# Moving the zero fill of the top-4 layer's slots from SyncE's queue to GpSimd's own queue in the first attention

## The reference, cut to what matters

```python
q = (x @ wq).reshape(Bq, Tq, N_KV, N_REP, HEAD_DIM)
k_lat = (x @ wk_down).reshape(Bq, Tq, N_KV, D_LAT)
v_lat = (x @ wv_down).reshape(Bq, Tq, N_KV, D_LAT)
...
scores = jnp.einsum('bqhrd,bkhd->bhrqk', q, k) * scale
scores = jnp.where(causal, scores, jnp.finfo(scores.dtype).min)
probs = jax.nn.softmax(scores, axis=-1)
y = jnp.einsum('bhrqk,bkhd->bqhrd', probs, v)
```

## Time and profile before

| | us |
|---|---|
| median of 3 runs | 1745.87 (1744.73 to 1747.52) |
| profiled execution | 1749.62 |
| its span on the core | 1747.7 |
| POOL busy in the span | 790.3 (45%) |
| PE / DVE / ACT busy in the span | 1187.7 / 1022.0 / 672.2 |
| first attention's units (first to last remainder on POOL) | 243.21 to 418.33 |

### The profile page before, as it was taken

One profiled execution on the slowest core, in us unless ns is written; L12 is line 12 of the kernel. 1 busy time (PEld: TensorE's weight loads), 2 busy tenths in 40 slices (PEclk: granted clock), 3 DMA queues, 4 the chain that ended last, 5 costly groups with the idle time before them and its releaser, 6 DMA issues.

```text
span 1747.7 us, 31813 instructions
## 1 busy us (share of the span) xinstructions
PE 1187.7 (68%) x10584; PEld 865.1 (50%) x10585; DVE 1022.0 (58%) x2671; ACT 672.2 (38%) x1035; POOL 790.3 (45%) x989
## 2 busy tenths in 40 slices
PE   2198568876199208598976448888885075989772
PEld 2198546654199203497962213444433034979620
DVE  6546656766546884142565757887766941335533
ACT  2154246664044102253531126766672022535310
POOL 0524435553423347666667522222200377666676
PEclk9999689997599559799997758999895587999986
DMA  9233134430133001454641100000000013646422
GB/s 363 65 94 111 38 104 144 151 123 2 36 95 87 25 24 49 130 191 161 192 128 49 42 14 2 2 0 0 0 1 1 24 49 120 198 156 199 145 60 62
DMA packets 100089, 150.10 MB, mean 86 GB/s; under 512 B 21520, under 2 KB 54928, under 8 KB 99216
## 3 DMA queue, kind: packets, MB, share of 16 engines
q1 hardware_dynamic: 58768, 75.30, 13.1%
q0 software_dynamic: 20480, 41.98, 8.1%
q10 hardware_dynamic: 20736, 31.47, 5.4%
HBM read 74.16 MB, written 74.45 MB: 85 GB/s over the span
## 4 chain that ended last, share of the span: by engine, by line
PE 26%; POOL 25%; DVE 16%; issue 14%; DMA 10%; SPq 4%; ACT 3%; DVEq 0%; ACTq 0%; POOLq 0%
POOL slots_top L624 15%; POOL AREA L1098 10%; PE PS L845 5%; DMA slots_top<-XN,ROW 4%; DMA AREA<-results_top,ROW 4%; SPq L1346 3%; PE PS L298 3%; PE PS L300 2%; PE PS L299 2%; PE PS L1789 2%; DVE AREA L1961 2%; DVE XN L407 2%; PE PS L1776 2%; PE PS L1764 2%; DMA query_rows<-AREA 1%
## 5 line engine op out<-in xcount | busy, mean ns | idle before, releaser
L624 POOL DMA_INDIRECT slots_top<-XN,ROW x320 | 317.4, 992 | 365.3 <-DVE ROW L578 225.0
L1098 POOL DMA_INDIRECT AREA<-results_top,ROW x320 | 304.6, 952 | 243.2 <-issue 87.8
L1009 DVE SCALAR_TENSOR_TENSOR AREA<-PS,AREA 128x512 f32<-128x512 f32 x96 | 66.4, 692 | 233.9 <-ACT AREA L983 209.8
L908 PE MATMUL PS<-WGU,AREA 128*128 x768 | 186.2, 386 | 0.0
L1961 DVE TENSOR_REDUCE AREA<-PS 128x4 f32<-128x1024 f32 x128 | 156.8, 1225 | 38.9 <-PE PS L1764 36.6
L1881 ACT ACTIVATE AREA<-PS,AREA 128x1024 f32<-128x1024 f32 x128 | 142.8, 1116 | 87.2 <-PE PS L1776 85.1
L908 PEld LDWEIGHTS PS<-WGU,AREA 128*128 128x128 f32 x768 | 141.4, 194 | 16.7 <-ACT AREA L972 0.7
L1379 POOL TENSOR_TENSOR AREA<-AREA 128x1536 f16<-128x1536 f32 x32 | 92.9, 2903 | 99.9 <-ACT AREA L1594 99.9
L417 PE MATMUL PS<-IDF,XN 128*128 128x128 f32 x192 | 48.7, 411 | 129.5 <-DVE XN L407 129.5
L930 PEld LDWEIGHTS PS<-WD,AREA 128*128 128x128 f32 x768 | 100.2, 191 | 12.7 <-DVE AREA L1004 8.2
L930 PE MATMUL PS<-WD,AREA 128*128 x768 | 102.0, 276 | 6.3 <-DVE AREA L1004 6.3
(11 more groups left out here) (257 smaller groups left out, 3147.4 us busy)
## 6 DMA issues: line engine op xcount, KB each, us to landing
AREA<-slots_top SPq DMA_DIRECT2D x96, 256.0 KB
results_top<-AREA ACTq DMA_DIRECT2D x96, 256.0 KB
slots_top<-ZERO SPq DMA_DIRECT2D x24, 512.0 KB, 3.1
AREA<-slots_top SPq DMA_DIRECT2D x48, 128.0 KB
results_top<-AREA ACTq DMA_DIRECT2D x48, 128.0 KB
AREA<-query_rows SPq DMA_DIRECT2D x48, 128.0 KB, 2.9
slots_top<-XN,ROW POOLq DMA_INDIRECT x320, 2.2
AREA<-results_top,ROW POOLq DMA_INDIRECT x320, 2.5
```

The costliest lines, as they stand in the source:

```text
L624: nc.gpsimd.indirect_dma_start(out=L.xs[q], out_offset=bass.IndirectOffsetOnAxis(ap=ROW[:, n:n + 1], axis=0), in_=XN[:, t * D:(t + 1) * D] ...
L908: ins = nc.tensor.matmul(o, XTF[:, v, j * P:(j + 1) * P], w, start=True, stop=True)
L1009: nc.vector.scalar_tensor_tensor(out=HF[:, v, :4 * P].rearrange("p (j h) -> p j h", h=P), in0=got, scalar=1.0 / SX, in1=HA[:, :4 * P].rear ...
L1098: nc.gpsimd.indirect_dma_start(out=slots[L.tag][u][:, c * D:(c + 1) * D], out_offset=None, in_=L.ys[g * GT // L.tiles], in_offset=bass.Ind ...
```

## The change

SP no longer issues the 24 pieces; POOL does, each behind the remainder of the unit of the same number. The tile, the destinations, the size of a piece and the semaphore stay. POOL's DMAs go through a queue of their own ("software dynamic" in the profile, q0) and SP's through another (q1).

```diff
@@ attn0_sync
                     max_row(t + 1)
                 if q_batch(t, 1) is not None:
                     q_write(q_batch(t, 1))
-                if 0 <= t < ZERO_PIECES["top4"]:
-                    zero_slots(sp, L1, t)
 
@@ attn0_pool
                 wait(pool, a_pv, u - 1)
                 nc.gpsimd.tensor_tensor(PB0[1][:, u % 2, :], PF[:, u % 2, :], PB0[0][:, u % 2, :], ALU.subtract
                                         ).then_inc(a_plo.sem, 1)
+                if u < ZERO_PIECES["top4"]:
+                    zero_slots(pool, L1, u)
```

## The result

| | before | with the change |
|---|---|---|
| median, 20 runs each | 1746.56 us | 1753.4 us |
| ratio, 95% interval | | 1.0043 (1.0026 to 1.0059) |
| span of the profiled execution | 1747.7 us | 1750.5 us |
| first to last remainder on POOL (start to start) | 172.2 us | 183.1 us |

The change made the kernel slower by 0.43%, some 7 us; 1744.7 and no change that can be told had been forecast, with a range that ended at 1750.0.

What follows compares the result with a forecast made beforehand. Mostly POOL's indirect DMAs bound the kernel; only the SP leg at 240 to 420 us could change. Terms -1.5 - 0.9 - 0.2 + 1.4 = -1.2 us gave 1744.7 us, 8-in-10 range 1737.5 to 1750.0.

Steps and rivals of the forecast that it cites:

- What bounds the kernel: Chain of waits: only the stage from 240 to 420 us can change, on a leg of SP's DMAs, then PE and ACT.
- 24 issues leave SP: First attention, SP's queue: of 24 zero pieces only three stand on the chain, so moving them gives -1.5 us.
- the three terms that a clean SP queue was given: SP's queue in the first attention: issues -1.5, landings of writes -0.9, rows of maxima -0.2 us.
- The first rival: First attention: SP is the pacemaker, 0.30 us per unit over 23 units, -6.9 us, time 1739.0; chance 0.35.
- Lighter queue: SP's queue without 512 KB pieces: seven query writes land sooner, -0.9 us, and rows of maxima, -0.2 us.
- POOL's DMAs at 0 us: 24 added issues on POOL, 1.3 us each, fit into 2.78 us free per unit, so cost 0.
- The zeros' bytes beside the queries: Seven query writes on the chain share DMA engines with pieces, 0.2 us each: +1.4 us, bounds 0 and +5.6.
- The price of full sharing: Delay of a query write that shares the DMA engines with a zero piece all the way: 0.8 us.
- Slower: contention on the whole SP leg: Zeros delay the write and again the read or rows, 0.8 + 0.8 us per leg: +8.6, time 1754.5; chance 0.11.
- POOL as the bound: First attention: POOL issues over 2.8 us would pace the stage; at 3.1 us +7.4 less 2.6, time 1750.7; chance 0.04.
- The sign of being wrong in kind: Time changing outside 240 to 420 us by more than a microsecond would show the prediction wrong in kind.
- the contention's bound for the writes alone: Upper bound of sharing by seven query writes: +5.6 - 2.6 = +3.0 us, used for the range's end at 1750.0.

Runs made afterwards that it cites:

- second trace of the kernel before: The kernel before, unchanged, traced again on the same chip as the change and SP behind the loop; first to last remainder 170.8 us, median 1744.12 us.
- SP behind the loop: Against the kernel before, SP issues all 24 zero pieces after the first attention's loop instead of in it; units 167.4 us, total 0.9985 (0.9967 to 1.0003).
- even kernel: Against the change, POOL issues two pieces behind each even unit, none behind odd ones; units 182.2 us, total 1.0057 (1.0028 to 1.0085) of the kernel before.
- second trace of the change: The changed kernel, unchanged, traced again on the same chip as the kernel before; units 181.0 us, total 1.0027 (1.0010 to 1.0044).
- kernel with odd units: Against the change, POOL issues two pieces behind each odd unit, none behind even ones; units 183.3 us, total 1.0042 (1.0018 to 1.0067) of the kernel before.
- the pair from one chip: The kernel before and the change, both unchanged, traced again on one chip; units 170.8 and 181.0 us, spans 1739.4 and 1749.1 us.

## Why the prediction was wrong

**What bounds the kernel.** Right. The SP leg that the prediction read (rows of maxima, write, landing, read, rows, landing, PE) is the chain in every trace, and most of the loss is in its two landings.

**24 issues leave SP, -1.5 us.** Right in kind and nearly in size: with no zeros at all the units take 167.4 us against 170.8 on one chip, and the three terms that a clean SP queue was given sum to 2.6 us. No run parts the three; in the second trace of the kernel before, five pieces stand on the chain, with 2.9 us. The first rival, 6.9 us and SP as the pacemaker, fell: taking all the zeros away gave half of it.

**Lighter queue, -0.9 and -0.2 us.** The values 2.30 and 1.7 us are what the kernels without zeros show, except beside a fetch of instructions (2.9 to 3.1 us with SP behind the loop), which the prediction rightly left in. But in the change this gain never came, since the pieces are only on another queue and not gone.

**POOL's DMAs at 0 us.** Right: 0.72 us an issue, nobody waits. The estimate of 1.26 us from the indirect DMAs was too high by 0.5, and this had a side effect: the piece is under way half a microsecond sooner than I had set it, and the lead of the write on which the next term rested was mostly gone.

**The zeros' bytes beside the queries, +1.4 us.** This is the step that failed. It was taken as 7 x 0.2 us, by a lead of the write of about 0.6 us, and only the write was counted. Measured, the landings on the chain grew by 4.0 us (writes) and 2.9 us (rows of maxima), together 6.9; the upper bound of the term was 5.6 for the writes alone. Two things were missed. The write does not lead: on the chain a piece is issued just ahead of one (278.40 and 278.99, 302.24 and 302.96). And the rows behind the read are exposed in the same way, as the odd and even kernels show. The rest of the stage's 10.9 us is in other steps of the chain (SP's issuing in the first pair); how much PE's lower clock adds is open.

The price of full sharing, 0.8 us for a write, was too low as well. It stood for 256 KB, as if the two moved side by side. The rows of the result show the whole piece ahead of the write, for 1.08 us; in the second trace of the change four writes that had a piece issued 0.6 us ahead of them and no fetch beside them landed after 3.36 to 3.38 us, 1.1 late, and those with the piece 1.2 us ahead after 2.78. Every write whose landing the two traces of the change give, and that was later than that, had a fetch of instructions beside it. The rule that I had weighed against my row, that engines take turns between queues packet by packet (the Trainium skill, DMA: Bandwidth & Descriptors, "Queues, rings and completion order"), was nearer the truth than my row: the sum by it ended at +3.0. The traces agree with it in part. In the even kernel the packets that the profile shows went one for one (92 and 88); in the change those of the piece all went first (96 and none). What decides between the two is open. (That no row of the trace before showed two queues at once was not quite so: the earlier trace rows has the fetch of instructions beside SP's queue, as the four late writes on that chain had.)

**The rivals.** "Slower: contention on the whole SP leg" is what happened, with its place (the landings of L1331 and of L1346 behind the read) and nearly its price: +8.6 us was worked out, +7 measured. It had 0.11. I held against it the lead of the write and the small size of the rows of maxima; but a DMA of 0.5 KB waits just as well, as the 3.54 us instead of 1.73 in the kernel with odd units show. POOL as the bound fell. The sign of being wrong in kind, a change of more than a microsecond outside 240 to 420 us, was set too tight: the first pair of traces differs there by 4.8 and 3.3 us and the pair from one chip by 0.6 and 1.2, which is what executions differ by.

**The range** ended at 1750.0, the contention's bound for the writes alone. With the rows of maxima at the same price it would have held the result.

## What to carry to other kernels

A bulk transfer on the same queue behind a transfer that someone waits for is ordered behind it; moved to another queue it can get ahead of it, and the time saved on the issuing queue is small when that queue sits in waits anyway. Before moving such an issue, write down which landings are on the chain, small ones included, and ask where each piece will be at each of them, with the legs free to shift. If there is a stretch in which the DMA engines are idle and nobody is waiting, put the bulk there, from an engine that is done.

## What the runs showed of the hardware

- A plain DMA of 128 x 2 stretches of 2 KB costs POOL 0.72 us of issue, 128 x 4 of 1 KB 0.76, and 128 x 8 of 512 bytes 0.90: less than an indirect one of 128 rows (0.96), and a quarter more for four times the stretches.
- On POOL's queue the packets are filled to 4 KB whatever the stretch (512 bytes, 1 KB or 2 KB: 144 packets per piece); on SP's queue the same piece had 272.
- 512 KB ahead of a 256 KB write on the same queue delayed it by 0.77 us nearly each time (3.07 against 2.30). On another queue, issued 0.6 us ahead of the write, they delayed it by 1.1 us, with all their packets ahead of the write's; where both began together the packets of 4 KB and of 1 KB alternated, and the write came 1.5 us late.
- With SP behind the loop, with no zeros about, the late writes on the chain (2.85 and 3.05 us instead of 2.30) had a fetch of instructions beside them, one packet of 16 KB on a queue of its own. With such a fetch and a piece on the other queue a write took as much as 5.07 us.
- PE's granted clock from 240 to 400 us was 0.96 with no zeros in the loop (SP's version), 0.93 and 0.96 in the two traces of the kernel before, 0.89 and 0.90 in the two of the change.
